# New orders of work on every engine for a decoder layer, self attention four batches ahead of cross attention, moments of x in groups of four

## The reference, cut to what matters

```
x = x + self_attention(layernorm(x))            # 16 heads of 8, relative position bias
x = x + cross_attention(layernorm(x), ctx, mask) # 16 heads of 8, masked by a given mask
x = x + ffn(layernorm(x))                        # 128 -> 512 -> 128
ffn(y): gate = silu(Q(y) Wg), up = Q(y) Wu, out = Q(gate*up) Wd
  Q(a) rounds a row to 127 steps of its largest magnitude; the W are rounded to -1, 0, 1 times a scale
```

## Time and profile before

| | |
|---|---|
| median of three runs | 460.03 us |
| the profiled execution, its own time | 459.56 us |
| its span, first to last instruction | 457.8 us |
| PE matmul busy | 400.1 us (87%) |
| DVE busy | 385.6 us (84%) |
| ACT busy | 360.1 us (79%) |
| POOL busy | 329.7 us (72%) |
| mean granted PE clock | 0.961 of full |

### The profile page before, as it was taken

How to read it: one execution, slowest core, us unless ns; L and a number is a source line. 1 busy time by engine, 2 the same in 40 slices (tenths; PEclk the granted TensorE clock), 3 DMA queues, 4 the chain that set the end, 5 groups by cost and what they waited for, 6 DMA issues and landing times. The chain is left out here.

```text
span 457.8 us, 16633 instructions
## 1 busy us (share of the span) xinstructions
PE 400.1 (87%) x5436; PEld 312.6 (68%) x5436; DVE 385.6 (84%) x1920; ACT 360.1 (79%) x962; POOL 329.7 (72%) x917
## 2 busy tenths in 40 slices
PE   3267879999999999999999999999999999877762
PEld 2245657777777777777877777778877777655430
DVE  4645367999999999999999999999999999887542
ACT  2214758899999999999999999999999998865542
POOL 5833766888888888888888888888888775654220
PEclk9998999999999999999999999999999999997665
DMA  6653577666665766667657665666566663423100
GB/s 189 163 145 100 134 190 183 174 150 174 167 172 145 190 167 174 147 188 177 170 148 195 174 175 153 173 170 169 153 167 180 156 170 82 101 78 77 29 7 12
DMA packets 100170, 67.18 MB, mean 147 GB/s; under 512 B 73269, under 2 KB 90421, under 8 KB 100085
## 3 DMA queue, kind: packets, MB, share of 16 engines
q1 hardware_dynamic: 98209, 64.08, 54.7%
q10 hardware_dynamic: 1876, 2.03, 1.4%
HBM read 46.08 MB, written 19.07 MB: 142 GB/s over the span
## 5 line engine op out<-in xcount | busy, mean ns | idle before, releaser
L857 DVE CUSTOM_DVE_ANT_0 biased<-bank,mask_bias 128x128 bf16<-128x128 f32 x512 | 112.7, 285 | 4.2 <-PE bank L1078 4.1
L862 DVE TENSOR_REDUCE neg_max_S<-bank 128x4 f32<-128x512 f32 x128 | 85.5, 675 | 21.6 <-PE bank L1078 20.7
L587 ACT ACTIVATE probs_S<-bank 128x512 f32<-128x512 f32 x128 | 72.7, 597 | 10.7 <-PE bank L1098 10.6
L587 ACT ACTIVATE probs_X<-bank 128x512 f32<-128x512 f32 x128 | 72.5, 591 | 7.3 <-PE bank L1098 6.7
L1078 PE MATMUL bank<-stack_k_S,stack_q_S 120*128 120x128 bf16 x512 | 51.0, 225 | 11.0 <-DMA stack_k_S<-scratch_S 10.1
L1098 PEld LDWEIGHTS bank<-stack_q_X,stack_k_X 74*128 74x128 bf16 x512 | 41.1, 100 | 16.7 <-issue 2.2
L1078 PEld LDWEIGHTS bank<-stack_k_S,stack_q_S 120*128 120x128 bf16 x512 | 39.1, 103 | 19.4 <-issue 11.1
L1098 PE MATMUL bank<-stack_q_X,stack_k_X 74*128 74x128 bf16 x512 | 51.4, 224 | 0.0
L1095 PE MATMUL bank<-ident_bf,mask_bias 128*128 128x512 bf16 x128 | 50.8, 397 | 0.0
L1078 PE MATMUL bank<-stack_k_X,stack_q_X 72*128 72x128 bf16 x512 | 45.5, 222 | 2.8 <-DMA stack_k_X<-scratch_X 1.8
L857 DVE DVE_READ_ACCUMULATOR2_ANT neg_max_X<- 128x1 f32 x512 | 42.2, 83 | 0.0
(11 more groups left out here) (165 smaller groups left out, 1190.8 us busy)
## 6 DMA issues: line engine op xcount, KB each, us to landing
stack_q_S<-scratch_S SPq DMA_DIRECT2D x32, 288.0 KB
stack_k_S<-scratch_S SPq DMA_DIRECT2D x32, 288.0 KB
stack_q_X<-scratch_X SPq DMA_DIRECT2D x32, 288.0 KB
stack_k_X<-scratch_X SPq DMA_DIRECT2D x32, 288.0 KB
scratch_S<-qk_parts_S SPq DMA_DIRECT2D x32, 192.0 KB, 2.9
scratch_X<-qk_parts_X SPq DMA_DIRECT2D x32, 192.0 KB, 2.5
scratch_S<-qk_parts_S SPq DMA_DIRECT2D x32, 64.0 KB, 1.6
ctxT<-ctx SPq DMA_DIRECT2D x8, 256.0 KB, 4.8
```

Source lines behind the costliest of these rows:

```text
L587: act.activation(probs[a][:, c, :], bank_b[c % 2][:, :], ACT.Exp).then_inc(sems["exp_" + a], 1)
L857: last = dve.tensor_tensor_reduce(biased[:, c, hh, :], quarter(bank_a[c % 2], hh), mask_bias[:, b % 2, :], -1.0, -2.0 * BIG, ALU.add, ALU.min,
L862: dve.tensor_reduce(neg_max[a][:, first_head(c):first_head(c) + 2 * HC - 1:2], bank_a[c % 2][:, :].rearrange("i (h j) -> i h j", h=HC), AX ...
```

## The change

It alters the order of nearly all work, and some instructions.

- Each engine has four lists: `fill` (self attention alone, five steps), `ramp` (six steps), `step` (28 steps) and `drain` (cross attention and F alone, 16 steps, of which the last have nothing left). Self attention's newest batch is four ahead of the cross attention's. An entry does every batch that has fallen due and that it has not done. PE's `step` list has all lags two higher than its `ramp` list, so its first two turns hold next to nothing.
- A wait for a PSUM bank's last reader comes from a record kept while the list is written (`take`), not from hand-written lists.
- The moments of x for S are taken for batches 0, 1 to 3, and then four at a time: statistics of all, then their aggregates; POOL does variance, negation and power for a group in one instruction each.
- `probs` has two buffers.
- `h_units` is one POOL instruction and not three. `hT_out` copies 256 float32 words, each two f16 numbers, and not 512 f16 numbers with a bias; the offset is taken off by a fifth matmul in `down`. `yT_out` and `quantise_h` have a constant bias in place of a column.
- The loads of x have a semaphore each; `rel_split` stands ahead of DVE's lists.

```diff
-STEPS = [(t, t) for t in range(-1, B + 10)]
+LEAD, RAMP, TAIL, LAGS = 4, 6, 6, 12
+MOMENTS = (0, 1, 4, 8, 12, 16, 20, 24, 28, 32)
...
+    def due(self, stage, lag, *key, n=B):
+        if self.newest[stage] is None:
+            return range(0)
+        first = self.begun.get((stage, key), 0)
+        end = max(first, min(self.newest[stage] - lag + 1, n))
+        self.begun[stage, key] = end
+        return range(first, end)
...
-        def run(step):
-            for s, x in STEPS:
-                step(Step(s, x))
+        def run(begun, fill, ramp, step, drain):
+            for s in range(-1, LEAD):
+                fill(Step(s, None, begun))
+            for x in range(RAMP):
+                ramp(Step(x + LEAD, x, begun))
+            for x in range(RAMP, B + TAIL - LEAD):
+                step(Step(x + LEAD, x, begun))
+            for x in range(B + TAIL - LEAD, B + TAIL + LAGS):
+                drain(Step(x + LEAD, x, begun))
...
+            def ln_group(st, lag):
+                for g in st.due("S", lag, "ln_group", n=len(MOMENTS) - 1):
+                    lo, hi = MOMENTS[g:g + 2]
...
+                    for b in range(lo, hi):
...
+                        dve.bn_stats(stats_s[:, b - lo, :], x_all[:, b, :]).then_inc(sems["stats_S"], 1)
+                    for b in range(lo, hi):
+                        dve.wait_ge(sems["stats_S"], b + 1)
+                        dve.bn_aggr(mv_s[:, b, :], stats_s[:, b - lo, :]).then_inc(sems["mv_S"], 1)
...
-                act.activation(hT[:].rearrange("p c s -> p (c s)"), bank_t[:, 0:256].bitcast(F16), ACT.Identity,
-                               bias=minus_round16[:, 0:1]).then_inc(sems["hT"], 1)
+                    copy(hT[:].rearrange("p c s -> p (c s)").bitcast(F32), bank_t[:, 0:256]).then_inc(sems["hT"], 1)
...
+                    last = pe.matmul(bank_t[:, 256:384], minus_offset[:], w_down_sum[:], start=False, stop=True)
```

More of the change, by code:

```diff
@@ new lines, in store @@
+            def store(st, lag):
+                for b in st.due("F", lag, "store"):
+                    if b < B - GROUP and b % GROUP != GROUP - 1:
+                        continue
+                    n = GROUP if b < B - GROUP else 1
+                    batches = slice(b + 1 - n, b + 1)
+                    sp.wait_ge(sems["res_F"], done(b))
+                    sp.dma_start(out[batches].rearrange("b s d -> s b d"), x_all[:, batches, :])\
+                        .then_inc(sems["out_stored"], 16)
@@ L365, in _, with drain @@
+            def drain(st):
+                stack_in("X", st, 1)
+                max_in("X", st, 2)
+                store(st, 4)
+                parts_out("X", st, 0)
+                parts_again("X", st, 0)
+            run(begun, fill, ramp, step, drain)
             sp.wait_ge(sems["out_stored"], 16 * (B // GROUP - 1 + GROUP))
@@ new lines, in ramp @@
+            def ramp(st):
+                attend_sums("S", st, 4)
+                attend_norm("S", st, 4)
+                ln_group(st, -2)
+                row_max("X", st, 3, 2)
+                row_max("X", st, 3, 3)
+                gate(st, 5)
+                ternary_weights(st, 4)
+                residual("S", st, 4)
+                gated(st, 5)
+                ln_stats("X", st, 0)
+                attend_sums("X", st, 4)
+                attend_norm("X", st, 4)
+                h_max(st, 5)
+                row_max("S", st, 2, 0)
+                row_max("S", st, 2, 1)
+                h_quantum(st, 5)
+                residual("X", st, 4)
+                h_inverse(st, 5)
+                h_scaling(st, 5)
+                ln_stats("F", st, 4)
+                ln_moments("X", st, 0)
+                ln_moments("F", st, 4)
+                row_max("S", st, 2, 2)
+                row_max("S", st, 2, 3)
+                row_max("X", st, 2, 0)
+                out_scaling(st, 5)
+                y_max(st, 4)
+                residual_ffn(st, 5)
+                y_unit(st, 4)
+                y_inverse(st, 4)
+                row_max("X", st, 2, 1)
@@ new lines, in step, with drain @@
+                h_quantum(st, 5)
+                residual("X", st, 4)
+                h_inverse(st, 5)
+                ln_stats("F", st, 4)
+                h_scaling(st, 5)
+                ln_moments("F", st, 4)
+                ln_stats("X", st, 0)
+                row_max("S", st, 2, 2)
+                out_scaling(st, 5)
+                ln_moments("X", st, 0)
+                row_max("S", st, 2, 3)
+            def drain(st):
+                y_max(st, 5)
+                row_max("X", st, 3, 0)
+                y_unit(st, 5)
+                residual_ffn(st, 6)
+                y_inverse(st, 5)
+                row_max("X", st, 3, 1)
+                row_max("X", st, 3, 2)
+                row_max("X", st, 3, 3)
+                gate(st, 5)
+                gated(st, 5)
+                attend_sums("X", st, 4)
+                attend_norm("X", st, 4)
+                h_max(st, 5)
+                h_quantum(st, 5)
+                residual("X", st, 4)
+                h_inverse(st, 5)
+                ln_stats("F", st, 4)
+                h_scaling(st, 5)
+                ln_moments("F", st, 4)
+                ln_stats("X", st, 0)
+                out_scaling(st, 5)
+                ln_moments("X", st, 0)
@@ L1021, in _ @@
+            rel_split()
+            run(begun, fill, ramp, step, drain)
         @block.tensor
         def _(pe):
+            begun = {}
             pe.wait_ge(sems["qkv_loaded"], 16 * 2)
```

1604 lines of the change are left out of this document (853 added, 751 removed).

## The result

The changed kernel took 462.72 us (median of 16 runs; 460.62 the fastest), the kernel before, run beside it, 460.47. The ratio is 1.0055, 95% interval 1.0031 to 1.008: slower by half a per cent, and the forecast was 438.8, 4.7% faster. The profiled execution has a span of 461.5 us where the forecast had 436.6.

What follows compares the result with a forecast made beforehand. DVE's instruction list was taken to bound the middle step. Start 83.0 + 26 x 11.2 + thin steps 54 + tail 8.4 = 436.6 us of span, 438.8 as a median of runs; range 429 to 455.

Steps and rivals of the forecast that it cites:

- the step is the sum of DVE's list, and the other engines follow it: Middle: DVE never waits long for others, so its list sets the step, 11.785 us before and 11.2 after.
- the start: From the beginning to the tanh of F batch 0: 83.0 us, before 86.47, bounds 78 and 92.
- the 26 steps: Full steps of the middle, between tanh of F batches 0 and 26: 11.2 us each.
- the five thin ones: Part-full steps after the full ones, five where there were four: 54 us, bounds 48 and 58.
- the short waits: Middle: part of DVE's idle time a step spent in short waits for others, 0.26 us of 0.44.
- The page's rule: DVE's pipeline is emptied after each operation anyway, so reordering gives nothing and the step stays near 11.8 us.
- the neighbours: Dependent instructions side by side on DVE cost 0.11 us more; pulling four pairs apart saves 0.44 a step.
- The first two: Rivals: only the ends gain, middle stays 11.785 (454.0 us, chance 0.20); only the middle gains, start's steps stay 10.15 (446.2, 0.09).
- Slower: Rival: in the middle, SP's queue makes the refill of S's stack late, step 12.4, 470 us; chance 0.09.
- My walk through the lists: Middle: one round with the rows' durations found each partner ready 0.2 to 0.5 us early at the tightest places.
- The mechanism: Start: `scores_b` directly behind `scores_a` cuts 3.7 us between refills to some 1.5, self attention steps 10.15 to 7.7.
- thin steps over 12 us: Sign that the forecast is wrong: thin steps this long would eat what the start gives.

Runs made afterwards that it cites:

- b1: Kernel before with only DVE's list changed, four dependent neighbours apart, moments of X behind the first maximum of S: steps of 12.48 us.
- b2: Kernel before with three dependent neighbours on DVE apart, moments of X left directly behind their statistics: steps of 12.08 us.
- g0: Changed kernel with store and bulk loads, `h_scaling`, v_aug X clearing and powers moved, `y_max` not: 1.3% faster than the kernel before.
- e5: Changed kernel with store, `load_x` and `load_c` directly behind `stack_in` S on SP: median 459.58 us, 26 full steps 296.48.
- e8: Changed kernel with bulk transfers, `h_scaling`, v_aug X clearing, powers and also `y_max` moved: good steps 11.40 us.
- g1: g0 with one more DVE instruction a step, unread statistics ahead of those of F: good step 11.21 us, where g0 had 11.17.
- e6: e5 with `h_scaling` behind the statistics of X, POOL's v_aug X clearing and group of means behind a split: good steps 11.16 to 11.24 us.
- e2: Changed kernel with moments of S and loads of x spaced, one group per four steps: 8.2 us slower than the changed kernel.
- e9: Changed kernel with POOL's power of a group of S behind the next batch's normalisation in `fill` and `ramp`: first tanh 92.97 us.
- e7: Changed kernel with the list of `step` used to the end in place of `drain`: 462.19 us.
- h1: g0 with ctx and mask loaded one batch a step directly behind `stack_in` S: median 454.89 us.

## Why the prediction was wrong

*The step that failed: "the step is the sum of DVE's list, and the other engines follow it."* DVE's lack of listed waits (two of 0.2 us in the stretch of the earlier trace rows, not one) and its full list led to it, but they don't say that a shorter list makes a shorter step. b1 and b2 are the direct test, and they went the other way by 0.7 and 0.3 us. What changed in them beside the gaps is where in the step each result is ready for POOL, PE and ACT, and the new waits are there. That I forecast 11.2 was in part chance: the changed kernel's good steps of 11.28 to 11.36 lie in my range of 11.05 to 11.4 and those of g0 at 11.17, but by the probes DVE's list is not what sets them.

*The terms of the sum that were too small:* the start (83.0, measured 93.06), the 26 steps (11.2 each, measured 11.637) and the five thin ones (54, measured 57.39). The tail was right. One working was off as well: of DVE's 11.77 us idle in the earlier trace rows, 2.15 lie in the last of the 27 steps, so the short waits were 0.19 us a step and not 0.26. No run takes the changed instructions back one at a time (the copy for `hT_out`, the fifth matmul, `h_units`, two buffers of `probs`), so what they bring stays open.

*The page's rule.* By the Trainium skill, page VectorE: DVE Perf Modes, section The DRAIN you can't avoid, I had worked out that the reordering is worth nothing. The rows of the changed kernel still show 0.08 of overlap without a dependence (`stats_F`, 166.78 and 0.29, the next at 166.99) and 0.03 of gap with one (`h_gate`, 162.51 and 0.68, `h` at 163.22), against the rule; the time that followed from it, no gain from the neighbours, came closer than mine, by waits between engines and not by the drain.

*The rivals.* None came as written. The first two (454.0 and 446.2) had no gain in one part; here the middle gained 4.2 us and the start and the end lost more. Slower had a chance of 0.09.

*The middle, 11.4 us.* By the runs: SP's order 6.1 (302.57 to 296.48 in e5). Of this, one step of 14.11 with a fall of the clock is 2.9, and that one is not surely SP's order: e8 and g1, with the new order, have such a step too (13.67, 13.86). The other 5.3 are, in e5, three long steps and the first two (3.1 above 11.2) and 0.1 in each good one (2.2). My walk through the lists took SP's queue as harmless apart from the refill of S. The slower rival had the right place, SP's order ahead of a refill, and the wrong stack: it is X's.

*The collision, and the moments.* I had not looked at what POOL does beside a DVE instruction of two SBUF inputs. It lengthens `h_scale` by 0.32 in nearly each step, but its removal in e6 took only 0.05 to 0.1 off the good ones. I also misread `due`: all nine groups are done in the first 72 us, not one in four steps, as this row of POOL's power shows (count, least, median and longest ns, first and last start):

```profile
L434 POOL TENSOR_TENSOR rstd_S<-veps_S,minus_half x9: 573/1038/1287, 5.2 to 72.2; 128x4 f32<-128x4 f32 x7, 128x1 f32<-128x1 f32 x1, 128x3 f32<-128x3 f32 x1
```

This took up to 0.3 us a step off the middle that the forecast didn't have, which e2 gives back (8.1 us), and it put six loads and eight lumps into the start.

*The start, 10.1 us.* Exp of S batch 0 at 34.05 and not 32.3: 1.4 of it from the clearing of v_aug X and POOL's group of means ahead of the split (32.69 in e8). The self attention steps were 9.57, 7.75 and 9.18 and not 7.7 each. The mechanism held in the second (PE waited 0.5 behind `keep_warm`, so that is hidden, as forecast). In the first, eight matmuls of the scores took 1.03 us and not 0.62. In the third, POOL had two powers in its list, 2.16 us, but e9 moved them and gained nothing. From there to the first tanh were 32.5 us and not 27.7, and on this way the clock fell. Windows of three us, PE's clock is the third column from the right:

```profile
65.00:68.00 3.00, 1.73 (x25) 1.43 (x17) 0.56 (x4) 1.63 (x6) 2.00 (x7) 1.00 0.71 206
68.00:71.00 3.00, 2.02 (x16) 1.16 (x14) 2.97 (x28) 1.00 (x5) 1.56 (x3) 0.72 0.51 118
71.00:74.00 3.00, 3.00 (x22) 2.88 (x23) 2.41 (x12) 1.56 (x5) 2.19 (x5) 0.50 0.77 211
74.00:77.00 3.00, 3.00 (x35) 2.38 (x33) 0.42 (x3) 2.12 (x7) 1.85 (x4) 0.64 0.18 52
```

PE was 1.73 and 2.02 busy of 3, then its clock went to 1.2 GHz. Seven profiled executions with all mends of the start have their first tanh at 90.9 in the mean (88.97 to 91.94), five without at 93.1 (91.14 to 94.67). The remaining 8 us against the forecast are the steps themselves; which order of the lists would remove them no run here shows.

*The thin steps, 3.4 us.* No cost of the drain's order shows (e7), and 3.4 us are within what executions differ by: the same kernel took 55.11 us in g0 and 61.41 in its second profile (g0_again). Here is the second of the thin steps in both:

```profile
399.49:410.03 10.54, 7.08 (x97) 5.18 (x100) 7.78 (x49) 6.96 (x17) 5.16 (x13) 1.00 0.30 84
```

```profile
396.47:409.87 13.40, 10.29 (x97) 7.53 (x100) 8.65 (x54) 7.01 (x18) 5.16 (x13) 0.71 0.25 67
```

The same 97 matmuls, 7.08 us at 2.4 GHz and 10.29 with a mean of 0.71. I had named thin steps over 12 us as what would eat the gain, and in the changed kernel two of five are (12.48, 12.74). What makes the clock fall in one execution and not in the other stays open.

## What to carry over

That an engine is full and never waits doesn't make it the bound; add 0.2 us of idle work to one engine at a time, look at the good steps, in more than one execution, and see which the step follows. Between engines in a ring, how early a result is ready for its reader can count for more than the gap it leaves on its own engine, as in b1. In an in-order queue of issues, place bulk transfers behind the refill that a reader waits for, not ahead of it.

## What the runs showed of the hardware

*POOL can hold DVE up.* In these rows a DVE instruction with two SBUF inputs (`h_scale`), and a cast of 256 float32 to bfloat16 in SBUF, end only when a POOL instruction that began before them is done: 0.47 and not 0.15 beside `qk_rest_X`, and 1.92 and not 0.29 beside a memset of 1.80 us:

```profile
10.68 1.92 DVE L914 CAST rel_parts<-rel_rest 128x256 bf16<-128x256 f32 x1
```

```profile
10.65 1.80 POOL L400 MEMSET v_aug_X<- 128x2048 f32 x1
```

The Trainium skill says so too, on the page SBUF — State Buffer, section SBUF: two separate sides: whichever of the two starts first has the shared ports for its whole instruction, for DVE instructions in a 2-port mode, or with two SBUF inputs where POOL's reads SBUF. The row of `h_scale` agrees. The memset reads nothing, so by this the cast would be the first kind, which no row can show. One pair is an exception to the rule: `down_scale`, of two SBUF inputs as well, took 0.14 while the power of F was running on POOL:

```profile
168.24 0.14 DVE L1059 TENSOR_TENSOR down_scale<-h_step,mean_w 128x1 f32<-128x1 f32 x1
```

```profile
168.12 0.58 POOL L461 TENSOR_TENSOR rstd_F<-veps_F,minus_half 128x1 f32<-128x1 f32 x1
```

*A power on POOL costs by the column*: 0.573 us for one, 0.887 for three, 1.107 in the mean for four. Grouping by four saves half, not three quarters.

*One late transfer costs twice.* In g0 PE waited 1.9 us for stack_k_X at 234 us, and then its clock fell:

```profile
230.00:233.00 3.00, 3.00 (x55) 2.40 (x53) 2.97 (x13) 2.97 (x9) 1.76 (x5) 1.00 0.49 149
233.00:236.00 3.00, 1.10 (x15) 0.82 (x14) 0.75 (x3) 1.43 (x6) 1.93 (x7) 1.00 0.79 232
236.00:239.00 3.00, 3.00 (x31) 2.54 (x30) 2.24 (x20) 2.20 (x5) 1.72 (x4) 0.66 0.71 186
```

The step took 14.73 and not 11.2; 1.9 are the wait, and the other 1.6 go with the lower clock. The ten runs of e5 lie near one line of that kind: 452.7 us at a mean clock of 0.970, 457 at 0.957, 462.9 at 0.936, some 3 us for 0.01. It is no law of the other versions: h1 took 454.9 us at 0.967 and 456.0 at 0.938.
